# Cross-attention and feed-forward on one core: the queries' rotary halves are projected as two blocks of four heads and moved into place by transfers

## The reference, cut to what matters

```python
kv_c = kv @ W_kvc                                   # 64 latents
q_c = q @ W_dq                                      # 96
q_nope = (q_c @ W_uq)                               # 16 heads of 128
q_rope = _rope((q_c @ W_qr), lq)                    # 16 heads of 64: [x1 cos - x2 sin, x1 sin + x2 cos]
k_nope, v = kv_c @ W_uk, kv_c @ W_uv
k_rope = _rope(kv_c @ W_kr, lk)                     # 64, shared by all heads
scores = (q_nope . k_nope + q_rope . k_rope) / sqrt(192)
scores = where(0 <= seg_id - k <= 8, scores, NEG)
x = x + tanh(g0) * (softmax(scores) @ v) @ W_o
x = x + tanh(g1) * bitlinear(layernorm(gelu(silu(bitlinear(layernorm(x))))))
```

## Time and profile before

| | us |
|---|---|
| median of 3 runs | 251.46 |
| profiled execution | 251.6 |
| its span | 249.8 |
| TensorE matmul busy | 210.2 |
| VectorE busy | 187.7 |
| ScalarE busy | 155.6 |
| GpSimd busy | 149.7 |

### The profile page before, as it was taken

How to read it: one execution, slowest core, us unless ns; L and a number is a source line. 1 busy time by engine, 2 the same in 40 slices (tenths; PEclk the granted TensorE clock), 3 DMA queues, 4 the chain that set the end, 5 groups by cost and what they waited for, 6 DMA issues and landing times.

```text
span 249.8 us, 4518 instructions
## 1 busy us (share of the span) xinstructions
PE 210.2 (84%) x1452; PEld 167.5 (67%) x1452; DVE 187.7 (75%) x430; ACT 155.6 (62%) x455; POOL 149.7 (60%) x222
## 2 busy tenths in 40 slices
PE   1799899999999999998998999899899746834453
PEld 1677788688978877886786888678678632513231
DVE  2587556689786679988988998898899842779761
ACT  2256627737557597759559875965887593849021
POOL 0415726639776469788787878778787832062630
PEclk9999999999999999999999999999999996775557
DMA  6999994000000000000000000000000000000001
GB/s 194 286 213 184 318 385 189 0 0 3 1 3 0 3 3 0 3 0 0 24 1 0 25 0 0 4 21 0 4 22 0 3 0 21 0 0 0 24 22 31
DMA packets 11357, 12.40 MB, mean 50 GB/s; under 512 B 3936, under 2 KB 10336, under 8 KB 11104
## 3 DMA queue, kind: packets, MB, share of 16 engines
q1 hardware_dynamic: 10432, 11.44, 16.6%
q10 hardware_dynamic: 896, 0.61, 0.8%
HBM read 11.00 MB, written 1.05 MB: 48 GB/s over the span
## 4 chain that ended last, share of the span: by engine, by line
PE 45%; DVE 19%; POOL 12%; issue 11%; ACT 9%; DMA 1%; DVEq 0%; SPq 0%; POOLq 0%
PE bank_pair L805 7%; PE bank_score L883 5%; PE bank_ff L920 4%; POOL h_small L430 4%; PE bank_lat L907 4%; PE bank_swap L808 3%; DVE z L1206 3%; PE bank_prob L895 3%; DVE h L1230 3%; POOL prob_room L485 3%; DVE neg_max L1289 3%; ACT prob_room L654 3%; PE bank_ff L959 3%; PE bank_ff L939 2%; POOL qcat L408 2%
## 5 line engine op out<-in xcount | busy, mean ns | idle before, releaser
L654 ACT ACTIVATE prob_room<-bank_score,neg_max 128x128 f32<-128x128 f32 x128 | 45.3, 369 | 23.5 <-DVE neg_max L1289 23.5
L485 POOL TENSOR_TENSOR prob_room<-prob_room,rsum 128x512 f32<-128x512 f32 x32 | 33.3, 1041 | 26.0 <-DVE rsum L1297 25.8
L406 POOL TENSOR_TENSOR qcat<-qcat,turned 64x256 f32<-64x256 f32 x32 | 30.8, 963 | 11.9 <-DVE turned L1141 11.8
L883 PEld LDWEIGHTS bank_score<-kcat,qcat 128*128 128x128 f32 x256 | 33.7, 192 | 2.3
L805 PE MATMUL bank_pair<-qcT,wcat 96*128 96x128 f32 x256 | 34.0, 276 | 0.0
L883 PE MATMUL bank_score<-kcat,qcat 128*128 128x128 f32 x256 | 33.7, 275 | 0.0
L642 ACT COPY probT_room<-bank_prob 128x512 f32<-128x512 f32 x32 | 19.0, 594 | 22.4 <-PE bank_prob L895 22.4
L920 PE MATMUL bank_ff<-m_sb,latT 128*128 128x256 f32 x128 | 31.9, 395 | 0.0
L805 PEld LDWEIGHTS bank_pair<-qcT,wcat 96*128 96x128 f32 x256 | 31.1, 192 | 0.4 <-DVE wcat L1126 0.2
L408 POOL TENSOR_TENSOR qcat<-qcat,turned 64x256 f32<-64x256 f32 x32 | 29.6, 924 | 2.5
L1137 DVE TENSOR_TENSOR qcat<-bank_pair,cst 128x512 f32<-128x512 f32 x32 | 21.6, 674 | 10.5 <-PE bank_swap L808 10.5
(11 more groups left out here) (163 smaller groups left out, 436.6 us busy)
## 6 DMA issues: line engine op xcount, KB each, us to landing
wo<-in_L_xattn_W_o SPq DMA_DIRECT2D x1, 2048.0 KB, 19.5
w_sb<-in_L_ffn_w SPq DMA_DIRECT2D x2, 1024.0 KB, 9.9
out_x<-y SPq DMA_DIRECT2D x8, 128.0 KB, 1.7
wuq<-in_L_xattn_W_uq SPq DMA_DIRECT2D x1, 768.0 KB, 11.5
ctx_all<-in_ctx ACTq DMA_DIRECT2D x2, 256.0 KB, 5.0
x_all<-in_x SPq DMA_DIRECT2D x2, 256.0 KB, 4.7
cst<-in_consts SPq DMA_DIRECT2D x1, 512.0 KB, 7.0
x_all<-in_x SPq DMA_DIRECT2D x1, 512.0 KB, 8.2
```

The lines of the kernel that those rows point to most:

```text
L406: nc.gpsimd.tensor_tensor(odd, odd, add_odd, ALU.add).then_inc(pair_half, 1)
L485: nc.gpsimd.tensor_tensor(p, p, rsum[:, k % 2, :].unsqueeze(2).broadcast_to([P, GROUP, kts * P]), ALU.mult).then_inc(prob_scaled, 1)
L654: last = nc.scalar.activation(prob_of(n, kts)[:, j, :], src[:, j, :], ACT.Exp, bias=neg_max[:, k % 2, j:j + 1], accum_out=esum[:, k % 2, j ...
L883: last = nc.tensor.matmul(bank[:, j * kts * P:(j + 1) * kts * P], qcat[:, k, hh // 2, hh % 2, :], kcat[:, b, hh % 2, 0:kts * P], start=Fal ...
```

## The change

- The rotary columns of W_qr are loaded whole (`wqr`, in the room of `tanh_z`) and copied into `wrope`: for each step one block of 128 columns with the first halves (32 values) of four heads and one with the second halves. `wnope` holds the folded latent part alone, both heads of a pair in 128 columns.
- `project` makes two matmuls of `wrope` into `bank_swap`, signals `rope_ready`, waits for `nope_copied` of the step before and makes two matmuls of `wnope` into `bank_pair`.
- VectorE makes one product of 128x512: each of the two blocks by the cosine and sine tables of both output halves (the table of constants grows from 4 to 6 blocks of 256 columns). GpSimd makes one addition of 128x256 into `rotated`.
- SP moves `rotated` into `qcat`: per step eight transfers of 32 partitions x 128 values, one for each head and half (`move_rope`). The stores of the tiles stand between the moves in SP's stream.
- ScalarE copies the latent parts from `bank_pair` into `qcat` (two copies of 64x256, `copy_nope`), behind the exponentials of each step.
- scores(n) waits for `nope_copied` and `rope_moved` of its step. AHEAD stays 2.

The diff, cut to its core:

```diff
+        wrope = sb("wrope", [QC, STEPS, 2, P])
+        wnope = sb("wnope", [QC, PAIRS, P])
+        product = sb("product", [P, 2, 2, 2, P])
+        rotated = sb("rotated", [P, STEPS, 2, P])
...
-            load(wcat[:, :, 0, KVC:P], wqr_pair[:, :, 0, :], "wqr0")
-            load(wcat[:, :, 1, 0:R], wqr_pair[:, :, 1, :], "wqr1")
+            load(wqr[:, :], W_qr, "wqr")
...
+            def move_rope(n):
+                k = n % STEPS
+                sp.wait_ge(rope_rotated, n + 1)
+                if n >= STEPS:
+                    sp.wait_ge(score_ready, n - STEPS + 1)
+                for hh in range(GROUP):
+                    for o in range(2):
+                        lo = (KVC if hh % 2 == 0 else 0) + o * half_r
+                        sp.dma_start(qcat[lo:lo + half_r, k, hh // 2, hh % 2, :],
+                                     rotated[hh * half_r:(hh + 1) * half_r, k, o, :]).then_inc(rope_moved[k], 16)
...
+            for n in range(N):
+                move_rope(n)
+                c = (n - 4 * STEPS - AHEAD) // STEPS
+                if c >= 0 and n == c * STEPS + 4 * STEPS + AHEAD:
+                    store(c)
+            for c in range((N - 1 - 4 * STEPS - AHEAD) // STEPS + 1, F):
+                store(c)
...
             def add_rope_step(f, k):
-                t = turned[:, k % 2, :].rearrange("p (j s) -> p j s", j=2)
-                add_rope(qcat[KVC:P, k, :, 0, :], qcat[0:R, k, :, 1, :], t[KVC:P, :, :], t[0:R, :, :], B + step_no(f, k))
+                n = step_no(f, k)
+                pool.wait_ge(rope_multiplied, n + 1)
+                if f > 0:
+                    pool.wait_ge(rope_moved[k], MOVED * f)
+                nc.gpsimd.tensor_tensor(rotated[:, k, :, :], product[:, k % 2, :, 0, :], product[:, k % 2, :, 1, :],
+                                        ALU.add).then_inc(rope_rotated, 1)
...
+            def copy_nope(f, k):
+                n = step_no(f, k)
+                act.wait_ge(nope_ready, n + 1)
+                if f > 0:
+                    act.wait_ge(score_ready, n - STEPS + 1)
+                src = bank_pair[:, 0:2 * P].rearrange("p (j s) -> p j s", j=2)
+                nc.scalar.copy(qcat[0:KVC, k, :, 0, :], src[0:KVC, :, :])
+                nc.scalar.copy(qcat[KVC:P, k, :, 1, :], src[KVC:P, :, :]).then_inc(nope_copied, 1)
...
-                        if f < F:
-                            exponentials(f, k, kts)
+                        exponentials(f, k, kts)
+                        if step_no(f, k) + AHEAD < N:
+                            copy_nope(*ahead(f, k))
...
             def project(f, k):
-                pe.wait_ge(pair_turned, s)
+                if n:
+                    pe.wait_ge(rope_multiplied, n)
+                else:
+                    pe.wait_ge(pair_turned, B)
+                for e in range(2):
+                    last = nc.tensor.matmul(bank_swap[:, e * P:(e + 1) * P], wrope[:, k, e, :], src, start=True, stop=True)
+                last.then_inc(rope_ready, 1)
+                if n:
+                    pe.wait_ge(nope_copied, n)
                 for j in range(2):
-                    for e in range(2):
-                        nc.tensor.matmul(bank_pair[:, (2 * j + e) * P:(2 * j + e + 1) * P], wcat[:, 2 * k + j, e, :], src,
-                                         start=True, stop=True)
-                for j in range(2):
-                    last = nc.tensor.matmul(bank_swap[:, j * P:(j + 1) * P], wswap[:, 2 * k + j, :], src, start=True, stop=True)
-                last.then_inc(pair_ready, 1)
+                    last = nc.tensor.matmul(bank_pair[:, j * P:(j + 1) * P], wnope[:, 2 * k + j, :], src, start=True, stop=True)
+                last.then_inc(nope_ready, 1)
...
-                pe.wait_ge(pair_done, B + n + 1)
+                if n == 0:
+                    pe.wait_ge(pair_done, B)
+                pe.wait_ge(nope_copied, n + 1)
+                pe.wait_ge(rope_moved[k], MOVED * (f + 1))
...
             def turn_step(f, k):
-                dve.wait_ge(pair_ready, s + 1)
-                if f > 0:
-                    dve.wait_ge(score_ready, step_no(f, k) - STEPS + 1)
-                nc.vector.tensor_tensor(qcat[:, k, :, :, :], bank_pair[:, :].rearrange("p (j e s) -> p j e s", j=2, e=2),
-                                        cos, ALU.mult)
-                dve.wait_ge(pair_done, max(B, s - 1))
-                nc.vector.tensor_tensor(turned[:, k % 2, :].rearrange("p (j s) -> p j s", j=2),
-                                        bank_swap[:, 0:S].rearrange("p (j s) -> p j s", j=2), sin, ALU.mult).then_inc(pair_turned, 1)
+                dve.wait_ge(rope_ready, n + 1)
+                if n >= 2:
+                    dve.wait_ge(rope_rotated, n - 1)
+                x = bank_swap[:, 0:2 * P].rearrange("p (e s) -> p e s", e=2).unsqueeze(1).broadcast_to([P, 2, 2, P])
+                nc.vector.tensor_tensor(product[:, k % 2, :, :, :], x, rot_tab[:, :, :, at:at + P],
+                                        ALU.mult).then_inc(rope_multiplied, 1)
```

More of the change, by code:

```diff
@@ L46, in shape_constants @@
     cos, sin = np.cos(ang).astype(np.float32), np.sin(ang).astype(np.float32)
-    one = np.ones((KVC, S), np.float32)
+    cos4, sin4 = np.concatenate([cos] * 4), np.concatenate([sin] * 4)
     c = np.zeros((P, CONSTS), np.float32)
@@ L50, in shape_constants @@
     c[:, IOTA:IOTA + S] = np.arange(S, dtype=np.float32)[None, :] + LOOKBACK / 2
-    c[:, COS:COS + S] = np.concatenate([one, cos, cos])
-    c[:, COS + S:COS + 2 * S] = np.concatenate([cos, cos, one])
+    for i, part in enumerate((cos4, -sin4, sin4, cos4)):
+        c[:, ROT + i * S:ROT + (i + 1) * S] = part
     c[:, SIN:SIN + S] = np.concatenate([-sin, sin, -sin, sin])
@@ L154, in build @@
         tanh_z = sb("tanh_z", [P, INNER])
+        wqr = tanh_z[0:QC, :]
         h_stats = sb("h_stats", [P, 12])
@@ L223, in build @@
         pair_done = sem("pair_done")
+        nope_ready = sem("nope_ready")
+        nope_copied = sem("nope_copied")
+        rope_ready = sem("rope_ready")
+        rope_multiplied = sem("rope_multiplied")
+        rope_rotated = sem("rope_rotated")
+        rope_moved = [sem(f"rope_moved{i}") for i in range(STEPS)]
         score_ready = sem("score_ready")
@@ L374, in _, with store @@
             out_v = out.rearrange("b (t p) d -> (b t) p d", p=P)
-            for f in range(F):
-                sp.wait_ge(y_done, f + 1)
-                sp.dma_start(out_v[f, :, :], y[:, :]).then_inc(out_stored, 16)
+            half_r = R // 2
+            def move_rope(n):
[8 more added lines that the diff above has]
+                                     rotated[hh * half_r:(hh + 1) * half_r, k, o, :]).then_inc(rope_moved[k], 16)
+            def store(c):
+                sp.wait_ge(y_done, c + 1)
+                sp.dma_start(out_v[c, :, :], y[:, :]).then_inc(out_stored, 16)
+            for n in range(N):
[5 more added lines that the diff above has]
+                store(c)
             sp.wait_ge(out_stored, 16 * F)
@@ L575, in _ @@
                                input_banks(i)[:, 1, :].rearrange("p (h c) -> p h c", h=4)).then_inc(wt_copied, 1)
+            def copy_nope(f, k):
[6 more added lines that the diff above has]
+                nc.scalar.copy(qcat[KVC:P, k, :, 1, :], src[KVC:P, :, :]).then_inc(nope_copied, 1)
+            for k in range(AHEAD):
+                copy_nope(0, k)
             act.wait_ge(in_sems["gate0"], 16)
@@ L1074, in turn_keys @@
                 dve.wait_ge(pair_ready, b + 1)
[L1075 to L1076 removed]
+                nc.vector.tensor_tensor(kcat[KVC:P, b, 0, :], bank_pair[KVC:P, 0:S], cos_tab[KVC:P, :], ALU.mult)
+                nc.vector.tensor_tensor(kcat[0:R, b, 1, :], bank_pair[0:R, 0:S], cos_tab[0:R, :], ALU.mult)
                 if b >= 2:
@@ L1106, in _ @@
             turn_keys(B - 1)
-            rope = R // 2
-            for e, o in ((1, 0), (0, KVC)):
-                dve.wait_ge(in_sems[f"wqr{e}"], 16)
-                nc.vector.tensor_copy(wswap[:, :, o:o + rope], wcat[:, :, e, o + rope:o + R])
-                last = nc.vector.tensor_copy(wswap[:, :, o + rope:o + R], wcat[:, :, e, o:o + rope])
+            dve.wait_ge(in_sems["wqr"], 16)
+            for e in range(2):
+                src = wqr[:, :].rearrange("k (t h x) -> k t h x", t=STEPS, h=GROUP)[:, :, :, e * (R // 2):(e + 1) * (R // 2)]
+                last = nc.vector.tensor_copy(wrope[:, :, e, :].rearrange("k t (h i) -> k t h i", h=GROUP), src)
             last.then_inc(wcopies, 1)
```

26 lines of the change are left out of this document (10 added, 16 removed).

## The result

The kernel after takes 279.03 us (median of 4 runs, 276.88 to 280.66), against 251.94 for the kernel before in the same session: a ratio of 1.106, with a 95% interval of 1.096 to 1.116. The forecast was 257.0 with a range of 249.5 to 264.5. The sign was right; the size was five times too small, and the time lies outside the range and beyond the dearest rival.

What follows compares the result with a forecast made beforehand. TensorE was taken to bound the early stretch, no engine alone the steady tiles. 251.6 us +5.4 (start) +2.5 (clock) +1.2 (early stretch) -3.5 (steady tiles) = 257.2, range 249.5 to 264.5.

Steps and rivals of the forecast that it cites:

- the dearest rival: Whole kernel: Rival 4, issues half a microsecond apart, giving 265 us; chance 0.22.
- GpSimd's addition: GpSimd, each step: one 128x256 addition takes 0.72 us (bounds 0.72 and 1.04), 0.75 us less per step.
- The landing of a move: SP's transfers, each step: the last lands 1.7 us after its issue by the store's row; 1.9 used in the path.
- The start: First scores: moves of steps 0 and 1 stand behind SP's late loads, scores(0) at 42.75 us, +5.4 us.
- a wait of the scores of step 5: Early stretch, step 5: scores wait for `qcat` 2 to 3 us, from 2.0 us of room against a 4.6 path.
- sign of having been too low: Steady tiles: the forecast is too low if steady scores wait for transfers in each step.
- The mis-sized term: SP, each step: eight issues at 0.38 us make a path of 4.6 us to the last landing (bounds 2.1 and 5.7).
- Rival 4: Whole kernel: issues half a microsecond apart, path 5.7 us, early steps lose 1.1 more each, tiles gain nothing: 265 us; chance 0.22.
- The failed step: Steps 2 to 13: 5.7 us saved, 6.9 given back in waits and copies, +1.2 net; steady tiles' 4.6 path just hidden.
- The clock: After the late start: TensorE, idle until 42.5 us, runs steps 0 and 1 partly at half rate, +2.5 us (0 to 4).
- Early saving: Steps 2 to 13: TensorE's shorter projections save 13x0.44 = 5.7 us.
- The steady tiles: Five tiles of 22.06 us: -0.6 to -0.7 each, transfers just hidden, -3.5 us in all (-7 to +1).

## Why the prediction was wrong in its size

**What held.** GpSimd's addition: taken at 0.72, 0.727 in the median (0.97 in the mean, since some beside VectorE's work take 1.7). ScalarE +23: +23.1. VectorE -10 to -13: -14.0, a little more. The landing of a move: taken as 1.9, 1.8. The start: +5.4 taken, +6.8 measured. A clock of 0.5 behind it, and a wait of the scores of step 5: as written. The forecast's own reason for a loss, a start that waits for transfers, is there too. So is its sign of having been too low: scores waited for moves in 15 of the 20 steps from 12 to 31.

**The mis-sized term: the issue.** I took 0.38 us, with 0.5 for the upper bound, from a lone store and from loads. Right behind one another the moves start 0.635 apart, so the path is 6.3 us and not 4.6, over my upper bound of 5.7. The row that misled was the store's 0.33: it was alone on its queue. In the kernel after the same store takes from 0.33 (alone, in the tail) to 0.58 (behind moves):

```profile
L400 SPq DMA_DIRECT2D out_x<-y x8: 332/459/582, 151.7 to 276.2; - x8
```

Rival 4 was the right one in kind, and it too stopped short. The sentence of the Trainium skill that initiating is usually small relative to the DMA ("DMA: Bandwidth & Descriptors", section "Issuing engines are not separate DMA queues") doesn't hold here: one issue is 0.59 of 1.8 us, and the eight of a step, 5.0 us, are nearly three times one landing.

**The failed step: what a longer path costs.** The sum gave the waits for transfers back one by one: +1.2 us for steps 2 to 13 and nothing in the steady tiles, where 4.6 was "just hidden". With 6.3 in place of 4.6 my own sum wouldn't have reached the result. By rival 4's slope (7.9 us for 1.1 us of path) 6.3 gives 257.2 + 1.7 x 7.2 = 269. Step 5 alone came out right: 2.0 us of room, 6.3 of path, so 4.3 late, and TensorE waited 4.14. But I had charged four steps of the early stretch and taken the others as covered. The path stands in a loop from the scores of one step to those of the step after next; each late score makes the next projection late, and the room that I had read in the timeline of before was not slack to be used once per step but the same slack for all. In steps 0 to 12 it cost +17.6, where I had 3.7 with the clock; in steps 12 to 31 +6.5, where I had -3.5. The kernel with three steps ahead shows it from the other side: same issues, one more step of room, +3.9 and -2.7. In the steady tiles the kernel without moves has 4.6 to 6.7 us from the addition's end to the scores, mostly under 6.3.

**What the sum never asked: SP's own rate.** I priced SP's issues as latency only. Eight issues and a share of a store are 5.3 us per step, more than the 4.7 that an early step takes; this alone puts the last scores near 207 us, without any loop. In the kernel after it hid behind the longer path; in the versions with three steps ahead it is what is left.

**The clock.** I charged it once, with 2.5 us. In steps 0 to 12 the traces have 387 matmul records without moves and 388 in the kernel after, for 50.25 and 57.70 us busy (the windows from the first scores to those of step 12, where the mean granted clock is 1.00 and 0.87). That is 7.4 us for the clock, since it fell again at 54, 72 and 100 us, after the waits. The 16.7 us by which the kernel after is longer there than the one without moves are these 7.4 and 9.3 of more idle time. A run with the waits and without the fall of the clock wasn't to be had, so how much of the idle time itself follows from the slower matmuls stays open.

**The start.** The size is near, the reason right only in part, so the hit was in part luck. I had the moves stand in line behind the loads in SP's queue. Another queue brought 1.1 us, and removing the late loads 3.5; what made them late were for the most part the busy DMA engines, and then the path itself, 6.4 us even with the engines free. The two causes overlap: 43.89 is not their sum.

**Early saving.** I booked 5.7 us for TensorE's shorter projections since it was busy 41.98 of 43 us. Without moves and copies steps 0 to 12 are 1.3 us shorter, with copies 0.9 longer. An engine that is full can have others right behind it. The copies are 2.2 us of it; which hand-over ends last there besides, once TensorE has less to do, I didn't settle.

**The steady tiles.** I took -0.6 to -0.7 for a tile, as -1.3 from VectorE and GpSimd and +0.7 from ScalarE; with the moves it is +1.6 (141.06 to 164.68). The kernel with small copies has -1.7 (20.36 against 22.06), the one with copies none: ScalarE's two copies cost 1.7 per tile, and I had them at half of that. ScalarE's share of the chain that ended last rose from 9% before to 27% without moves; I had followed the copies to tanh at k=1 and to nothing else.

**Account,** by medians: 251.3; all of the change but its moves -1.6 (the work saved -11.3, the copies +9.5, from two sessions); their traffic +1.1; one awaited transfer per step +6.3, almost all of it at the start; eight instead of one, the path from 2.1 to 6.3 us, +21.9; in all 279.

## What to carry to other kernels

Count DMA issues as instructions of an engine, back to back, and take their price from rows where several stand one behind another: here 0.64 us each, so that eight of 16 KB are nearly three times as long as the landing of the last, while one with the bytes of all eight took 0.47. Then add up all issues of the queue and hold them against the whole stretch: here 171 to 174 us against 160. Where a new hand-over stands in a loop of a pipeline, add up the whole loop (all its stations, over the number of steps it runs ahead) and compare it with the period; where the loop is longer every step pays, and a step more of distance may give most of it back. Work taken from the fullest engine counts only up to the next engine, and what is put on another counts in full if it stands ahead of its links in the chain.

## What the runs showed of the hardware

- An issue of a 16 KB transfer from SBUF to SBUF over 32 partitions takes SP 0.51 us as the first of a row and 0.59 behind another, 0.635 from start to start; one of 128 KB over 128 partitions, alone, 0.465; from GpSimd 0.496, the first of four and the later ones alike; a store 0.33 alone and 0.58 right behind moves; a broadcast load 0.58 right behind a move and 0.43 to 0.68 behind another load. More bytes and partitions didn't make an issue dearer, a move ahead of it on SP's queue did.
- 256 such moves and the stores between them kept SP's queue for 171 to 174 us, whether scores waited for them or not.
- A transfer from a queue without loads of its own took 5.2 us to land while the loads of another kept the DMA engines full, 2.0 otherwise.
- TensorE's granted clock fell to 1.2 GHz at 38 to 40 us, when TensorE had been idle since 36, and again at 72 to 78 and 100 to 102 us, where it stood idle for some 2 to 4 us; the mean from 37 to 80 us was 0.76. Eight matmuls of the scores that took 0.89 us then took 1.71.
- 31 GB/s of moves between tiles of SBUF (a DMA share of 0.13) left the engines' busy times as they were.
